# Unread products between the prologue's score pairs, and another layout of the first block's filler work

## The reference

```python
qh = heads(layernorm(x) @ Wq.T); kh = groups(ctx @ Wk.T); vh = groups(ctx @ Wv.T)
score = einsum('bhqd,bhkd->bhqk', qh, repeat(kh)) / sqrt(16)
out = softmax(score) @ repeat(vh)
x = x + tanh(g_xattn) * (out @ Wfc.T + bfc)
h = layernorm(x)
x = x + tanh(g_ffn) * (mlp(h, shared 2048) + mlp(h, routed 256) * top2_weight_sum(h @ router.T))
```

## Time and profile before

| | |
|---|---|
| median of three runs | 888.81 us (888.25 to 889.77) |
| the profiled execution | 890.05 us, of it the span of the trace 887.7 us |
| mean granted TensorE clock | 0.990 of full |
| busy, share of span | TensorE 97%, VectorE 72%, GpSimd 54%, ScalarE 38% |
| PE, by 40 slices, in tenths | 8689999999999889999999999999999999999998 |
| granted clock, by 40 slices, in tenths | 9889999999999999999999999999999999999999 |

### The profile page before, as it was taken

The page is one execution under the profiler, slowest core; times in us unless marked ns, Lnnn a source line. Parts: engine busy times, 40 slices in busy tenths (PEclk is TensorE's granted clock), DMA queues, the critical chain, the costliest instruction groups (busy, mean ns, idle before and its releaser), DMA issues.

```text
span 887.7 us, 14887 instructions
## 1 busy us (share of the span) xinstructions
PE 860.1 (97%) x4923; PEld 642.5 (72%) x4923; DVE 635.8 (72%) x1085; ACT 337.2 (38%) x636; POOL 477.8 (54%) x485
## 2 busy tenths in 40 slices
PE   8689999999999889999999999999999999999998
PEld 6445665665565447888888888888788888888886
DVE  7789899889889966666556655679665566656565
ACT  4186576667657852122112211344211121112111
POOL 2313004001203999787668666954966696678640
PEclk9889999999999999999999999999999999999999
DMA  7763342432432113121112111211311112111102
GB/s 274 232 175 105 127 121 61 149 116 78 131 107 74 38 28 93 48 72 47 47 47 71 47 47 47 72 47 65 115 59 48 47 52 66 47 47 47 47 1 95
DMA packets 43609, 71.88 MB, mean 81 GB/s; under 512 B 6064, under 2 KB 21936, under 8 KB 43312
## 3 DMA queue, kind: packets, MB, share of 16 engines
q1 hardware_dynamic: 43568, 71.34, 25.5%
HBM read 55.33 MB, written 15.73 MB: 80 GB/s over the span
## 4 chain that ended last, share of the span: by engine, by line
PE 84%; DVE 11%; issue 2%; ACT 1%; DMA 1%; SPq 0%; DVEq 0%; ACTq 0%
PE bank L1293 24%; PE bank L1295 23%; PE bank L1294 23%; DVE mcol L906 5%; PE bank L1353 4%; PE bank L1378 4%; PE bank L1368 3%; PE bank L1298 2%; PE bank L1399 1%; DVE oN L1038 1%; ACT probs L761 1%; DVE oB L1028 1%; DVE x_l L1256 1%; DVE aT_l L881 0%; DMA q_scr<-qx_l 0%
## 5 line engine op out<-in xcount | busy, mean ns | idle before, releaser
L1293 PE MATMUL bank<-x_l,w_h 128*128 128x512 f32 x504 | 197.3, 391 | 0.3 <-DVE c L1116 0.3
L1294 PE MATMUL bank<-x_h,w_l 128*128 128x512 f32 x504 | 196.2, 389 | 0.0
L1295 PE MATMUL bank<-x_h,w_h 128*128 128x512 f32 x504 | 196.2, 389 | 0.0
L906 DVE TENSOR_REDUCE mcol<-bank 128x2 f32<-128x512 f32 x256 | 164.7, 671 | 24.8 <-PE bank L1353 24.3
L620 ACT ACTIVATE hT_h<-bank 128x512 fp32r<-128x512 f32 x72 | 43.1, 599 | 355.9 <-DVE bank L1231 347.2
L761 ACT ACTIVATE probs<-bank 128x512 f32<-128x512 f32 x256 | 138.9, 596 | 73.3 <-PE bank L1368 71.7
L572 POOL TENSOR_TENSOR w_l<-raw,w_h 128x512 fp32r<-128x512 f32 (+1 forms) x144 | 161.9, 1157 | 2.9
L1128 DVE SCALAR_TENSOR_TENSOR xa<-bank,tgf,xa 128x512 f32<-128x512 f32 x128 | 96.2, 751 | 77.7 <-PE bank L1295 77.5
L1293 PE MATMUL bank<-dn_l,hT_h 128*128 128x512 f32 x288 | 112.0, 389 | 0.0
L1294 PE MATMUL bank<-dn_h,hT_l 128*128 128x512 f32 x288 | 112.0, 389 | 0.0
L1295 PE MATMUL bank<-dn_h,hT_h 128*128 128x512 f32 x288 | 112.0, 389 | 0.0
(11 more groups left out here) (149 smaller groups left out, 1340.6 us busy)
## 6 DMA issues: line engine op xcount, KB each, us to landing
raw<-w_gu SPq DMA_DIRECT2D x36, 512.0 KB, 3.3
dnraw<-w_dn SPq DMA_DIRECT2D x36, 256.0 KB, 2.6
q_st<-q_scr SPq DMA_DIRECT2D x64, 128.0 KB, 2.7
q_scr<-qx_h SPq DMA_DIRECT2D x16, 256.0 KB, 2.2
q_scr<-qx_l SPq DMA_DIRECT2D x16, 256.0 KB, 2.2
q_st<-q_scr SPq DMA_DIRECT2D x64, 64.0 KB, 2.7
out<-xa SPq DMA_DIRECT2D x16, 256.0 KB, 2.0
cx_raw<-ctxT SPq DMA_DIRECT2D x14, 256.0 KB, 3.0
```

The lines of the kernel that those rows point to most:

```text
L906: v.tensor_reduce(at[:, :, qt], sm_bank(n, s, u)[:, :].rearrange("p (r k) -> p r k", r=2), AX.X, ALU.max).then_inc(max_ok, 1)
L1293: mm(out, a_h, b_l, start=start, stop=False, skip_group_check=onto)
L1294: mm(out, a_l, b_h, start=False, stop=False, skip_group_check=onto)
L1295: return mm(out, a_h, b_h, start=False, stop=stop, skip_group_check=onto)
```

## The change

The prologue turns V of the second batch too, and 32 unread products (the table WARM, 128x512 each, into PJ[1]) stand after this and after each of the eight score pairs of steps 0 and 1. In block 0 only:

- context chunks 2 and 3 are loaded in step 1, not 2, and split by GpSimd in step 2, not 3; the load of the first feed-forward weight goes from step 1 to step 2 of the SyncE queue;
- ScalarE: `wfc_high` from (1,1), (2,1) to (1,5), (2,7); `cx_high` to (1,1), (1,3), (2,1), (2,5); `v_copy` and `k_high` from (3,7) to (3,3); three `q_high` moved;
- VectorE: the statistics of the last x from steps 2 and 3 to 5 and 6, `aggregates` from step 4 to 7, `norm_rows` from 5 to the end of 7, `k_low` from (4,1) to (3,5), the first `f_sum` from (6,7) to (7,2), `f_stats` from (7,4) to (7,6); two `q_low` moved;
- TensorE: the 32 parts lie in steps 2 to 7 as 6, 4, 6, 5, 5 and 6; one of each step (`block0_first`) stands ahead of `mt_job`, the others (`block0_rest`) behind it.

The diff, cut to its core:

```diff
@@ SyncE, GpSimd @@
-                    if s in (0, 2) and not last:
-                        load_cx(t + 1, s)
-                        load_cx(t + 1, s + 1)
+                    if s in ((0, 1) if first else (0, 2)) and not last:
+                        c = 2 * s if first else s
+                        load_cx(t + 1, c)
+                        load_cx(t + 1, c + 1)
...
-                    if s == 1 and first:
+                    if s == 2 and first:
                         sp.dma_start(raw0[:, A11:, :].rearrange("p a k -> p (a k)"), w_gu[0, :, :]).then_inc(in_gu[0], 16)
...
+                    if s in ((1, 2) if first else (1, 3)):
+                        c = 2 * s - 2 if first else s - 1
+                        cx_low(t + 1, c)
+                        cx_low(t + 1, c + 1)
+                    if first and s == 7:
                         deviations(2)
@@ ScalarE @@
             vt_copy(0, 0)
+            vt_copy(0, 1)
             q_high(0, 3)
...
-                        if first and (s, u) in ((1, 1), (2, 1)):
+                        if first and (s, u) in ((1, 5), (2, 7)):
                             wfc_high(s - 1)
-                        if s == 1 and u in (1, 5):
-                            cx_high(nx, u // 4)
+                        if s == 1 and u in ((1, 3) if first else (1, 5)):
+                            cx_high(nx, u // 2 if first else u // 4)
...
-                        if (s, u) in ((2, 7), (3, 1)):
-                            cx_high(nx, s)
+                        if (s, u) in (((2, 1), (2, 5)) if first else ((2, 7), (3, 1))):
+                            cx_high(nx, 2 + u // 5 if first else s)
+                        turns = ((4, 3), (4, 7), (5, 7), (7, 3)) if first else ((4, 3), (5, 3), (6, 1), (7, 3))
@@ VectorE @@
-                        if first and s in (2, 3) and u in (4, 7):
+                        if first and s in (5, 6) and u in (4, 7):
                             dve.wait_ge(in_x[BLOCKS - 1], 16)
-                            tile_stats(T // P - TILES + 2 * (s - 2) + u // 7)
-                        if first and s == 4 and u == 0:
+                            tile_stats(T // P - TILES + 2 * (s - 5) + u // 7)
+                        if first and s == 7 and u == 0:
                             aggregates(BLOCKS - 1)
-                        if first and s == 5 and u == 0:
+                        if first and s == 7 and u == 7:
                             norm_rows(2)
...
-                        if s in (6, 7) and u == 7:
-                            f_sum(t, 0, s - 6)
+                        if (s, u) in (((7, 2), (7, 7)) if first else ((6, 7), (7, 7))):
+                            f_sum(t, 0, u // 7 if first else s - 6)
-                        if s == 4 and u == 1:
+                        if (s, u) == ((3, 5) if first else (4, 1)):
                             k_low(nx)
+                        turns = ((4, 5), (5, 1), (6, 1), (7, 5)) if first else ((4, 5), (5, 5), (6, 3), (7, 5))
@@ TensorE @@
+            WARM = (6, 1, 4, 4, 6, 3, 2, 4, 2)
             pe.wait_ge(k_rd[0], 64)
+            pe.wait_ge(k_lo, 1)
+            vt_job(0, 1)
+            pe.wait_ge(vt_cp, 1)
+            keep_warm(WARM[0], PJ[1])
             pe.wait_ge(q_rd[0], 64)
             for v in range(UNITS // 2):
                 sm_pair(0, 0, v, 0, 0)
+                keep_warm(WARM[1 + v], PJ[1])
             pe.wait_ge(q_lo, 3)
             mt_job(0, 0)
             pe.wait_ge(q_rd[1], 64)
             for v in range(UNITS // 2):
                 sm_pair(1, 1, v, 0, 1)
+                keep_warm(WARM[5 + v], PJ[1])
...
+            def block0_first(t, s, v):
+                nx = t + 1
+                if (s, v) == (2, 1):
+                    pe.wait_ge(x_lo, TILES * nx + 4)
+                    kv_part(nx, 0, 0)
+                if (s, v) == (3, 1):
+                    kv_part(nx, 0, 3)
+                if (s, v) == (4, 1):
+                    q_part(nx, 0, 2)
+                if (s, v) == (5, 1):
+                    pe.wait_ge(q_lo, CHUNKS * nx + 1)
+                    q_part(nx, 2, 0)
+                if (s, v) == (6, 1):
+                    f_part(t, 0, 0, 1)
+                if (s, v) == (7, 1):
+                    q_part(nx, 3, 2)
+            def block0_rest(t, s, v):
+                nx = t + 1
+                if (s, v) == (2, 1):
+                    kv_part(nx, 1, 0)
+                    kv_part(nx, 0, 1)
+                    kv_part(nx, 1, 1)
+                if (s, v) == (2, 3):
+                    kv_part(nx, 0, 2)
+                    kv_part(nx, 1, 2)
+                if (s, v) == (3, 1):
+                    kv_part(nx, 1, 3)
+                if (s, v) == (3, 3):
+                    pe.wait_ge(v_cp, nx + 1)
+                    q_part(nx, 0, 0)
+                    q_part(nx, 0, 1)
...
+                if (s, v) == (7, 1):
+                    q_part(nx, 3, 3)
+                    pe.wait_ge(f_add, TILES * t + 1)
+                    f_part(t, 0, 1, 0)
```

More of the change, by code:

```diff
@@ L767, in body @@
                             a_high(n - 1, (s - 1) % CHUNKS, (s - 1) % STEPS // CHUNKS, 2 * t + (s - 1) // CHUNKS)
-                        if (s, u) == ((0, 5) if last else (2, 3)):
+                        if not first and (s, u) == ((0, 5) if last else (2, 3)):
                             vt_copy(t, 1)
@@ L1097, in body @@
                             continue
-                        if s in (6, 7) and u == 7:
-                            f_sum(t, 0, s - 6)
-                        if s == 7 and u == 4:
+                        if (s, u) in (((7, 2), (7, 7)) if first else ((6, 7), (7, 7))):
+                            f_sum(t, 0, u // 7 if first else s - 6)
+                        if s == 7 and u == (6 if first else 4):
                             f_stats(t, 0, 0)
@@ L1393, in x2_job, with keep_warm @@
                 last.then_inc(x2_tr, 1)
-            def keep_warm(count):
+            def keep_warm(count, to=bank[5]):
                 for _ in range(count):
-                    last = mm(bank[5][:, :], k_st[:, 0, 0, 0:P], k_st[:, 0, 0:2, :], start=True, stop=True)
+                    last = mm(to[:, :], k_st[:, 0, 0, 0:P], k_st[:, 0, 0:2, :], start=True, stop=True)
                 return last
+            WARM = (6, 1, 4, 4, 6, 3, 2, 4, 2)
             pe.wait_ge(consts, CONSTS)
@@ new lines, in block0_rest @@
+            def block0_rest(t, s, v):
[13 more added lines that the diff above has]
+                    q_part(nx, 0, 1)
+                if (s, v) == (4, 1):
+                    q_part(nx, 0, 3)
+                    pe.wait_ge(k_lo, nx + 1)
+                    q_part(nx, 1, 0)
+                if (s, v) == (4, 3):
+                    for c4 in range(1, DC):
+                        q_part(nx, 1, c4)
+                if (s, v) == (5, 1):
+                    q_part(nx, 2, 1)
+                if (s, v) == (5, 3):
+                    q_part(nx, 2, 2)
+                    q_part(nx, 2, 3)
+                    pe.wait_ge(q_lo, CHUNKS * nx + 2)
+                    pe.wait_ge(wfc_ok, 2)
+                    f_part(t, 0, 0, 0)
+                if (s, v) == (6, 1):
+                    f_part(t, 0, 0, 2)
+                if (s, v) == (6, 3):
+                    f_part(t, 0, 0, 3)
+                    pe.wait_ge(q_lo, CHUNKS * nx + 3)
+                    q_part(nx, 3, 0)
+                    q_part(nx, 3, 1)
+                if (s, v) == (7, 1):
+                    q_part(nx, 3, 3)
+                    pe.wait_ge(f_add, TILES * t + 1)
+                    f_part(t, 0, 1, 0)
+                if (s, v) == (7, 3):
+                    for c4 in range(1, DC):
+                        f_part(t, 0, 1, c4)
@@ L1478, in body @@
                                 f_part(t - 1, 1, 1, 2)
-                        if not last:
+                        if first:
+                            block0_first(t, s, v)
+                        elif not last:
                             if s == 3 and v == 1:
@@ L1488, in body @@
                                 pe.wait_ge(q_lo, CHUNKS * nx + 2)
-                                if first:
-                                    pe.wait_ge(wfc_ok, 2)
                                 f_part(t, 0, 0, 0)
@@ L1553, in body @@
                             x_job(nx, 2 + v // 2)
-                        if s == 2 and v == 1:
+                        if s == 2 and v == 1 and not first:
                             pe.wait_ge(x_lo, TILES * nx + 4)
                             vt_job(t, 1)
+                        if first:
+                            block0_rest(t, s, v)
+                        if first and s < STEPS - 1:
+                            continue
                         if s == 2 and v == 3:
@@ L1559, in body @@
                             kv_part(nx, 0, 0)
-                            if not first:
-                                pe.wait_ge(f_add, TILES * t)
+                            pe.wait_ge(f_add, TILES * t)
```

(4 more changed lines are left out.)

16 lines of the change are left out of this document (6 added, 10 removed).

## The result

The changed kernel takes 892.87 us in the median of five runs (890.82 to 893.42), the kernel before 888.64 (five runs, 888.25 to 889.77). The ratio is 1.0042, with a 95% interval of 1.003 to 1.0053: slower by 0.4%, where 885.3 was forecast. The profiled execution took 893.42 us (span 891.0) against 890.05 before, +3.37. Step 8 starts at 122.63 us, before it did at 119.21, +3.42, and takes 8.34 us in both; so all of it is lost ahead of that.

A forecast was written before the change was run, and what follows sets the result against it. Before about 120 us slow TensorE bound step 0, ScalarE step 1, VectorE steps 2 and 4, TensorE 5 to 7. Terms summed to -3.45, say -3.5, from the median 888.81: 885.3 us, range 883.7 to 888.2 (forecast's own 883.9 to 887.0).

The forecast's parts named there:

- what they buy: the clock stays at 2.4 GHz: Prologue: the 32 unread products, 7.3 us at full clock, keep TensorE's clock from falling at about 36 us.
- Rival C: Clock falls all the same before about 38 us and step 0 starts 3.0 later: +1.9, 890.7 us; chance 0.07.
- the port: Step 2: VectorE's two-input operations meeting GpSimd's splits cost 1.06 a meeting; half of one counted, step 2 at 9.6, 0.
- The bias sums on GpSimd stay: Step 4: GpSimd's bias sums keep their place, with what they stretch, while VectorE falls from 10.4 to 8.6.
- The row of maxima: SyncE queue, end of step 1: the row is issued behind the context loads, so step 2 waits: +0.4 (0 to 1.0).
- The start: Ahead of step 0: the hole in the maxima shrinks from 1.29 to some 0.9, step 0 starts at 44.4: -0.5.
- step 0: Step 0 of block 0: at full clock 7.2 us instead of 9.33: -2.1 (bounds 6.5 and 8.6).
- step 1 without the wait: Step 1 of block 0: ScalarE's same operations in another order, 8.7 us; 9.1 against 8.61 with the wait, +0.5.
- steps 3: Step 3: four parts again; VectorE loses a statistic and gains the low part of K: 8.1 us, 0.
- 4: Step 4: VectorE's 10.4 falls to 8.6, TensorE with six parts is next at 9.4: -1.0.
- 5 and 6: Steps 5 and 6: five parts, 8.9 us each instead of 9.32 and 9.35: -0.9 together (0 to -1.3).
- 7: Step 7: VectorE gains the aggregates and first f_sum: 9.9 us instead of 9.56, +0.35 (bounds 9.6 and 10.6).

The follow-up runs named there:

- e3: Changed kernel with the loads of context chunks 2 and 3 issued behind the row of maxima in step 1: 893.11 us, ratio 1.0048 to the kernel before.
- e5: Changed kernel with both edits, context loads behind the row of maxima and bias sums held until step 3 is done: 890.96 us, ratio 1.0017.
- e6: e5 with the low part of the output weight's first half made at (2,3), not (2,6), on VectorE: 890.14 us, ratio 1.0015.
- e2: Changed kernel without the 32 unread products, layout and turning of V kept: 891.05 us, ratio 1.003 to the kernel before.
- e4: Changed kernel with GpSimd's bias sums for block 1 held until step 3 is done: 890.17 us, ratio 1.001 to the kernel before.
- e8: Changed kernel with 18 more unread products in steps 0 and 1 of block 0: 891.78 us, ratio 1.0031 to the kernel before.
- e7: e6 with 18 more unread products in steps 0 and 1 of block 0: 888.86 us, ratio 1.0 to the kernel before.
- e10: e6 without the queue edit, so the context loads stand ahead of the row of maxima as in the changed kernel: 890.13 us.
- e11: e6 without any of the 32 unread products: 889.6 us, ratio 1.0003 to the kernel before.
- e9: e6 with five more unread products in steps 0 to 2, each in a hole of TensorE: 886.79 us, ratio 0.9972 to the kernel before.
- e1: Kernel before with the 32 unread products alone, its old layout of block 0 kept: 888.7 us, ratio 0.9997 to the kernel before.

## Why the prediction was wrong

**The step that failed first** is "what they buy: the clock stays at 2.4 GHz". The products hold it only as long as they run. Behind them come steps 0 and 1, with 6 to 7 us of TensorE work each in 7.4 and 8.8. My argument that step 1 had kept 2.4 GHz with 6.96 of 8.61 rested on one execution that came out of dense work. Rival C asked whether the clock falls before 38 us, and put its price into the prologue; the fall came after the prologue and struck at step 2. There it costs over two fifths of its length: 5.6 us at half clock made 2.5 us in the changed kernel, 6.8 made 2.9 in e3, against 9.64 at full clock. In e5 a fall of 6.8 us in step 0 made 1.7 (9.03 against 7.36 in e6). Before, 17.1 us made about 2.0, all in step 0, as TensorE waited for maxima in the rest. I had asked whether the clock falls, and not what runs when it does.

**The second** is the port, priced as half of one meeting of 1.06, "one of two". The meeting is not a chance: `cx_high` of chunk 3 at (2,5) releases GpSimd just as VectorE comes to (2,6), and in all six kernels that have it there (the changed one, e2, e3, e4, e5, e8) the weight's low part took 2.31 to 2.33. The prediction's sentence on the Trainium skill ("SBUF — State Buffer", Who interferes with whom) had put this very operation at 1.1 us more, and that is what e4 to e6 measured (step 3, 9.43 to 8.28). The rows bear the rule out, and both ways: whoever starts second waits for the whole first instruction, VectorE in the changed kernel with 1.24 of waiting and 1.08 of work, GpSimd in e7.

**The third** I did not see. "The bias sums on GpSimd stay" is wrong: they were held until step 4 only because `deviations` stood ahead of them on GpSimd and waited for the aggregates. With `deviations` moved to step 7 they start 10 us earlier, on top of VectorE's two-input operations. Of a step that is moved, what it held back counts too. With the second this is 2.1 us (e7 against e8).

**The row of maxima** was the right mechanism. Its issue was forecast 6.05 us into the step and came at 6.1 in the changed kernel, e2 and e10. It then took 3.3, 3.0 and 3.9 us until step 2 could start, where I had said at most 3.52; the cost was 0.6, 0.35 and 1.2 against 0.4 forecast (0 to 1.0). The q_st read was late as well (0.94 in e10), which I had left out; that the loads' traffic did it is likely and not shown. In step 2 I took away one statistic of VectorE, where the trace of the kernel before has two (68.39 and 71.91); as TensorE became the bound there, nothing hung on it.

**The start**, forecast 0.5 earlier, came out equal (44.94 to 44.92). The hole in the maxima did shrink, from 1.28 to 0.88:

```profile
39.52 3.81 DVE L910 TENSOR_REDUCE mcol<-bank 128x2 f32<-128x512 f32 x6 [0.88 <-PE bank L1358]
43.51 1.29 DVE L910 TENSOR_REDUCE mcol<-bank 128x2 f32<-128x512 f32 x2 [0.17 <-PE bank L1358]
```

What it gave was lost again: 0.14 inside the six maxima (3.81 against 3.67 in the earlier trace rows), 0.17 ahead of the last two, and the rest where the eight no longer run on without a break. The groups of products are longer than I had them, as the first of a group takes 0.43 and not 0.23. And the 0.2 for the pair of step 2 at full clock was not there: from it to step 0 it is 0.60 both times (44.32 and 44.34). From the first scores to step 0 it is 12.4 before and 12.3 in all the others, with products or without; so the products won nothing there. Ahead of the scores the six lost up to a microsecond where q_st landed in time: e2 and e11, without them, start step 0 at 43.58 and 43.72, the eleven executions with them at 44.37 to 46.01 (some of this is the scatter of the start, as two executions cannot tell).

**Right** were, by e6: step 0 (7.2; 7.36), step 1 without the wait (8.7; 8.82), steps 3 (8.1; 8.28), 4 (9.4; 9.34), 5 and 6 (8.9; 8.77) and 7 (9.9; 9.80); the 0.2 more in step 8 did not come (8.34 in both). So the terms behind the start were right for a kernel with a mended queue, a free port and a full clock: 886.3 to 886.5 in two of ten executions. That is 3.6 to 3.7 us under the profiled execution of the kernel before, against which I had summed, but only 2.6 to 2.7 under the median on that chip (889.04). I had taken the -3.5 over to the median, and no execution of any kernel here reached 885.3; the lowest took 885.69 (e9).

The account of the changed kernel against the forecast start of step 8 (122.63 to 115.6, 7.0 us): start 0.5; step 0 1.0, of it 0.9 by the fall at 47.6; step 1 0.3; step 2 2.5, by the clock; step 3 3.1, of it 1.6 the port with the bias sums, 0.2 a step too short in the forecast, and the rest, by subtraction, the clock; steps 4 to 7 -0.4.

**Open** is what exactly tips the clock. The same kernel (e6) fell in eight executions of ten and not in two, and e1, with thin steps too, fell at other places. That what TensorE does in steps 0 and 1 decides it is shown by e7 and e8, each beside its twin without the 18 products (filled, no fall in the profiles and a mean clock of at least 0.997 in all fifteen executions). e9 agrees with seven of nine at full clock, but e6 ran on another chip; the only run with the port edits and the 32 products on e9's chip, e10, had none in ten, without the queue edit. Which hole decides it is not shown, nor what made the third fall of the changed kernel, as e2, e3 and e8 have the same stretch of the port at full clock.

## What to carry to other kernels

A TensorE clock held by unread products is held only while they run: look at what comes next, and if that is thin, put a product into each hole there (read from a profile at full clock; a single one costs about 0.43 us, more than it is worth where there is no hole, as e7 showed), or leave the low stretch where TensorE waits anyway. Price a fall by the work that stands behind it. Products placed ahead of a wait for a transfer are free only as long as the transfer is late. And when an operation is moved on an engine's queue, look at what it had held back, and at which instruction of the port's other user starts in the same microsecond.

## What the runs showed of the hardware

- An unread 128x512 product costs 0.23 us in a run of its kind, but the first behind another kind of product about 0.43 (the two rows of e7); four together took 1.13 in the changed kernel, which is 0.43 and three of 0.23.
- The granted clock of the same kernel differs from execution to execution: e6 had 0.990 to 1.000, with 886.3 to 891.3 us; the kernel before, whose low stretch lies mostly in waits of TensorE, only 0.987 to 0.992, with a spread of 2.3 us on the same chip (1.6 to 3.2 on the others).
- A two-input operation of VectorE that starts just behind one of GpSimd waits for it to end: 2.31 to 2.33 us for 1.08 of work, in six kernels. The other way round GpSimd waits: 2.25 us where it takes 1.28 (e7).
